# Gate and up as seven products per pair of chunks instead of eight, residual kept in DRAM

## What is computed

```
x = _layernorm(x + attn(x, Wq, Wk, Wv, Wo))
Wg = (gate_w - 128) * gate_scale[:, None]      # Wu and Wd in the same way
g = einsum('bsh,ih->bsi', x, Wg)
u = einsum('bsh,ih->bsi', x, Wu)
h = silu(g) * u
x = _layernorm(x + einsum('bsi,hi->bsh', h, Wd))
```

## Time and profile before

| | us |
|---|---|
| median of 3 runs (1772.68 to 1777.62) | 1775.47 |
| the profiled execution | 1769.1 |
| its span, slowest core | 1767.6 |
| TensorE busy in it | 1736.1 |
| VectorE, GpSimd, ScalarE busy | 545.4, 328.2, 263.8 |
| first gate/up half, with the wait at its start | 444.5 |
| second gate/up half | 441.9 |

### The profile page before, as it was taken

The page is one execution under the profiler, slowest core; times in us unless marked ns, Lnnn a source line. Parts: engine busy times, 40 slices in busy tenths (PEclk is TensorE's granted clock), DMA queues, the critical chain, the costliest instruction groups (busy, mean ns, idle before and its releaser), DMA issues.

```text
span 1767.6 us, 22037 instructions; the slowest of 8 cores (1762.0 to 1767.6 us)
## 1 busy us (share of the span) xinstructions
PE 1736.1 (98%) x8156; PEld 790.6 (45%) x8156; DVE 545.4 (31%) x950; ACT 263.8 (15%) x469; POOL 328.2 (19%) x459
## 2 busy tenths in 40 slices
PE   6999999999999999999999999999999999999997
...
PEclk9999999999999999999999999999999999999999
...
GB/s 145 179 95 143 143 144 161 171 178 118 85 83 78 78 72 73 83 76 106 25 90 122 81 74 36 73 82 77 79 72 72 83 78 106 23 138 155 51 72 119
DMA packets 146503, 173.27 MB, mean 98 GB/s; under 512 B 107872, under 2 KB 110048, under 8 KB 146272
## 3 DMA queue, kind: packets, MB, share of 16 engines
...
q10 hardware_dynamic: 144, 0.26, 0.0%
HBM read 266.21 MB, written 8.39 MB: 155 GB/s over the span
## 4 chain that ended last, share of the span: by engine, by line
PE 92%; DMA 3%; SPq 2%; POOL 1%; DVE 1%; issue 1%; ACT 0%; DVEq 0%; ACTq 0%; POOLq 0%
PE ps L324 25%; PE ps L336 25%; PE ps L354 20%; PE ps L379 5%; PE ps L303 4%; PE ps L267 4%; SPq L794 2%; DMA wk<-wk_os 2%; PE ps L255 2%; PE ps L192 2%; PE ps L284 2%; PE ps L237 1%; PE ps L239 1%; PE ps L200 1%; PE ps L214 1%; PE ps L206 1%
## 5 line engine op out<-in xcount | busy, mean ns | idle before, releaser
L324 PE MATMUL ps<-y1T,wgu 128*128 128x512 bf16 x2048 | 462.9, 379 | 2.2 <-DMA y1T<-y1b 2.2
L336 PE MATMUL ps<-y1T,wgu 128*128 128x512 bf16 x2048 | 462.9, 379 | 0.0
L324 PEld LDWEIGHTS ps<-y1T,wgu 128*128 128x128 bf16 x2048 | 200.3, 98 | 244.1 <-issue 2.6
L336 PEld LDWEIGHTS ps<-y1T,wgu 128*128 128x128 bf16 x2048 | 200.3, 98 | 241.8
L659 ACT ACTIVATE sil<-ps,gus 128x512 f32<-128x512 f32 x128 | 87.8, 687 | 1004.9 <-PE ps L324 775.9
L354 PE MATMUL ps<-wd,h_lo 128*128 128x512 bf16 x1024 | 222.4, 379 | 0.0
L506 DVE SCALAR_TENSOR_TENSOR h_hi<-ps,gus,sil 128x512 bf16<-128x512 f32 x64 | 48.0, 751 | 354.5 <-PE ps L336 354.5
L354 PEld LDWEIGHTS ps<-wd,h_lo 128*128 128x128 bf16 x1024 | 100.0, 98 | 121.1 <-issue 0.4
L506 DVE SCALAR_TENSOR_TENSOR h_lo<-ps,gus,sil 128x512 bf16<-128x512 f32 x64 | 48.1, 751 | 343.2 <-PE ps L336 342.4
L747 POOL DMA_DIRECT2D wgu<-wu_is x62 | 32.8, 528 | 641.7 <-PE ps L324 619.6
L354 PE MATMUL ps<-wd,h_hi 128*128 128x512 bf16 x640 | 139.4, 379 | 0.0
...
## 6 DMA issues: line engine op xcount, KB each, us to landing
wgu<-wg_is POOLq DMA_DIRECT2D x64, 512.0 KB, 6.1
wgu<-wu_is POOLq DMA_DIRECT2D x64, 512.0 KB, 5.1
wd<-wd_bs POOLq DMA_DIRECT2D x52, 512.0 KB, 5.4
wq<-wq_os POOLq DMA_DIRECT2D x16, 512.0 KB, 33.9
wo<-wo_bs POOLq DMA_DIRECT2D x16, 512.0 KB, 7.3
...
y<-Sx SPq DMA_DIRECT2D x14, 512.0 KB, 2.8
wdf<-wd_bs POOLq DMA_DIRECT2D x12, 512.0 KB, 9.1
```

Of the source, the lines that this page charges most:

```text
L324: mm = t.matmul(bank(2 * (u % 4)), wgu[(2 * i) % 5][:, 128 * k:128 * k + 128], y1T[:, T * k + 512 * tt:T * k + 512 * tt + 512], start=(k = ...
L336: mm = t.matmul(bank(2 * (u % 4) + 1), wgu[(2 * i + 1) % 5][:, 128 * k:128 * k + 128], y1T[:, T * k + 512 * tt:T * k + 512 * tt + 512], st ...
```

## The change

**Seven products.** Two chunks, 2p and 2p+1, are a pair; with the two token halves (tiles 0 to 3 and 4 to 7) and the two halves of the 2,048 input features (columns 0 to 1023 and 1024 to 2047) gate and up are each a product of 2x2 blocks. Eight block products are replaced by seven on sums and differences of blocks (Strassen's scheme in the form with shared sums). A block product has 8 matmuls instead of 16 for a full one. `pair(p)` has 14 products, x = 0 to 13, seven for gate and seven for up in turn (m = 0 and 1), each in bank (14p+x) mod 8.

**Token sums.** `y1T` is replaced by seven tensors: yB11 and yB22 (blocks), yD21 and yD12 (differences), ySc, ySb and ySa (sums of tiles j and j+4). The normed tiles are written as 128x1024 pieces: ScalarE writes a block (`stg`) and norms one half of `Sx` in place, VectorE norms the other half, GpSimd subtracts (L996), and VectorE and GpSimd then make twelve sums `sts`. SyncE transposes 28 pieces of 1,024 columns instead of 8 of 2,048.

**Weight sums.** Slabs stay in bf16 with 128 subtracted, so their sums are whole numbers that bf16 holds exactly. For each pair VectorE centers four slabs `raw` and makes six sums of 128x1024 (`sum_q`, `sum_r`, `sum_p`) for the next pair, GpSimd four differences (`dif_v`, `dif_u`); they go round in twelve buffers `cmb`.

**Result sums.** ScalarE copies products 0, 1, 4 and 5 into SBUF (`x4`, `x3`), VectorE adds the others to them from PSUM (`c21`, `c12`, `e4`, `c11`, `c22`, two each), GpSimd makes the sums between (`s34`, `f11_f22`, six of 128x512 f32), ScalarE the four `sil`, and VectorE the four `h` blocks (`hprod`), now with both inputs in SBUF.

**Buffers.** Since the sums need space, the normed residual is written to a DRAM scratch `y1s` by ScalarE's queue after the norm, is read and rewritten in 128x512 pieces (`ybk`) during the first down part by SyncE's queue, and is read back into SBUF (`Sy`) after the second gate/up half. The down slabs have four buffers, which are the four `raw` of the odd pairs. In `down` TensorE waits for h step by step.

```diff
+    y1s = nc.dram_tensor("y1s", [NQT, 128, D], F32)
...
+    wd = [at(f"wd{i}", 2048, BF16, raw_off[4 + i] * KB) for i in range(4)]
...
+            def product(p, x, w, y):
+                for k in range(8):
+                    mm = t.matmul(bank((14 * p + x) % 8), w[:, 128 * k:128 * k + 128],
+                                  y[:, 512 * k:512 * k + 512], start=(k == 0), stop=(k == 7))
+                mm.then_inc(pe_m, 1)
+
+            def pair(p):
+                for m in range(2):
+                    t.wait_ge(ve_cw, 4 * p + m + 1)
+                    empty(p, m)
...
+                    product(p, m, raw[rslot(p, m, 1)][:, 1024:2048], yD21)
...
+                for m in range(2):
+                    t.wait_ge(po_cb, 4 * p + 2 + m + 1)
+                    empty(p, 12 + m)
...
+                    product(p, 12 + m, cmb[cslot(p, QU, m)], ySa)
...
+            def sum_q(p, m):
+                v.wait_ge(ve_cw, 4 * p + m + 1)
+                cfree(v, p, QQ + m)
+                v.tensor_tensor(cmb[cslot(p, QQ, m)][:, :], quarter(p, m, 2, 1), quarter(p, m, 2, 2),
+                                ALU.add).then_inc(ve_cb, 1)
...
+            def e4(p, m):
+                v.wait_ge(pe_m, 14 * p + 8 + m + 1)
+                v.wait_ge(po_s34, 2 * p + m + 1)
+                v.tensor_tensor(x4[m][:, :], x4[m][:, :], bank((14 * p + 8 + m) % 8), ALU.add).then_inc(ve_e, 1)
...
+            def hpair(p, slab):
+
+                more = p + 1 < NP
+                if more:
+                    cen(p + 1, 0)
+                    cen(p + 1, 1)
+                    sum_q(p + 1, 0)
+                    sum_q(p + 1, 1)
+                c21(p, 0)
+                c21(p, 1)
+                hprod(p, 0)
...
+                hprod(p, 2)
+                if slab is not None:
+                    cen_wd(slab)
+                c22(p, 0)
...
+            def s34(p, m):
+                g.wait_ge(ac_s3, 2 * p + m + 1)
+                g.wait_ge(ve_c21, 2 * p + m + 1)
+                g.tensor_tensor(x4[m][:, :], x4[m][:, :], x3[m][:, :], ALU.add).then_inc(po_s34, 1)
+
+            def f11_f22(p, m):
+                g.wait_ge(ve_e, 2 * p + m + 1)
+                g.wait_ge(ve_c12, 2 * p + m + 1)
+                g.wait_ge(po_s34, 2 * p + m + 1)
+                g.tensor_tensor(x3[m][:, :], x4[m][:, :], y12[m][:, :], ALU.subtract).then_inc(po_f11, 1)
+                g.wait_ge(po_f11, 2 * p + m + 1)
+                g.tensor_tensor(x4[m][:, :], x4[m][:, :], y21[m][:, :], ALU.subtract).then_inc(po_f22, 1)
+
+            def sums(p):
+                dif_v(p, 0)
+                dif_v(p, 1)
+                dif_u(p, 0)
+                s34(p, 0)
+                s34(p, 1)
+                dif_u(p, 1)
+                f11_f22(p, 0)
+                f11_f22(p, 1)
+
+            def slabs_free(p):
+
+                g.wait_ge(pe_m, 14 * p + 6)
+                g.wait_ge(ve_cb, 6 * p + 6)
+                g.wait_ge(po_cb, 4 * p + 4)
...
+            for p in range(HP):
+                sums(p)
+                slabs_free(p)
+                if p < HP - 1:
+                    for x in range(4):
+                        gu(p + 2, x)
+            for w in range(WA):
+                wds(w)
...
+            for d in range(4):
+                for j in range(NQT):
+                    if d > 0:
+                        sy.wait_ge(st_yb[j // 4], 64 * d)
+                    sy.dma_start(ybk[j][:, :], y1s[j, :, 512 * d:512 * d + 512]).then_inc(ld_yb, 16)
+                for j in range(NQT):
+                    sy.wait_ge(ve_da, 8 * d + j + 1)
+                    sy.dma_start(y1s[j, :, 512 * d:512 * d + 512], ybk[j][:, :]).then_inc(st_yb[j // 4], 16)
```

More of the change, by code:

```diff
@@ L342, in down @@
+            def down(lo, hi, q):
                 for d in range(lo, hi):
```

554 lines of the change are left out of this document (385 added, 169 removed).

## The result

The changed kernel takes 1850.3 us (median of 4 runs, 1849.0 to 1851.2), the kernel before 1775.1 beside it: ratio 1.0423, 95% interval 1.0405 to 1.0441. It is slower by 75 us. In some executions the cores of one die show a lower granted clock and take longer; the ratios leave these out, and so do the times given for e2_memset and e5_slab_early, two each.

A forecast was written before the change was run, and what follows sets the result against it. The kernel before was taken as bound by TensorE, the changed one by VectorE and GpSimd excluding each other. 1769.1 + 59.9 + 31.1 = 1860.1, with 5 added 1865 us; range 1728 to 1925, the forecast's own 1812 to 1925.

The forecast's parts named there:

- case (e): The forecast itself: a gate/up pair takes 28 to 31 us, slower, 1812 to 1907 us, likeliest 1865; chance 0.60.
- A pair of 29.6 us: Gate/up: VectorE and GpSimd exclude each other and bind a pair in turn at 29.6 us; TensorE idles a fifth.
- rival (b): Gate/up: GpSimd's bf16 difference takes 1.27 us, not 2.4; pair 25.2 us, time 1728 to 1733; chance 0.10.
- (d): Gate/up: VectorE's bf16 sum takes 1.2 us, not 0.61; pair 33 us, time 1960; chance 0.08.
- each one that waits going next: Pair layout: VectorE and GpSimd alternate, giving 29.6 us; 26.1 if VectorE's consecutive instructions keep their turn, 30.8 if GpSimd's do.
- (c): Gate/up: VectorE keeps its turn in runs; pair 26.1 us, time 1755 to 1760; chance 0.10.
- Second half, +31.1: Second gate/up half: 5 us down tail, 15 pairs (444), last pair 24; 473 against 441.9 us.
- First half, +59.9: First gate/up half: pair 0 ends at +57, 14 pairs of 29.6, last pair 33; 504.4 against 444.5 us.
- The waits for the first down slab: Last pair of each gate/up half: down slabs come late; first down matmul at 33 us, in the second half 24.
- (a): Gate/up: no exclusion that matters, TensorE stays the bound at 24.2 us a pair; time 1688 to 1693; chance 0.12.
- The idle costs nothing more: Gate/up: despite TensorE's idle time the granted clock stays at nine tenths or more of 2.4 GHz; no added time.
- The residual's trips: Start and down stages: the residual's DRAM traffic costs nothing; if cover goes, one wait of some 5 us in second down.

The follow-up runs named there:

- e2_memset: Changed kernel with GpSimd's four weight differences per pair replaced by memsets of the same tiles, differences left out of the result: 1820.5 and 1814.9 us, ratio 1.0245.
- e5_slab_early: Changed kernel with the next pair's or first down slabs issued by GpSimd before `f11_f22` instead of behind it: 1800.4 and 1801.0 us.
- e10: e5_slab_early with each GpSimd weight difference replaced by two memsets in a row, differences left out of the result: 1730.5 us, ratio 0.9739.
- e4: Changed kernel with the norm's one-element product `nm` rewritten to have one SBUF tensor input: 1852.3 us, ratio 1.0438.
- e7: e6_all with VectorE's order in the first pair rewritten, pair 0's combinations and h products ahead of centering pair 1's slabs: 1732.7 us, ratio 0.9750.
- e11: e7 with two of pair 1's four slabs held back behind the ySa transposes: 1727.3 us, ratio 0.9711.
- e3_dif_dve: Changed kernel with the four weight differences of a pair made by VectorE instead of GpSimd: 1797.1 us, ratio 1.0125.
- e9: Changed kernel with the residual's loads for the second down stage issued block by block, not all at once: 1854.4 us, ratio 1.0441.
- e6_all: Changed kernel with weight differences on VectorE, slabs issued before f11/f22, the norm's product with one tensor input, and residual loads block by block: 1725.0 us, ratio 0.9708.

## Why the prediction was right, and which of its steps were not

The time (1850.3 against 1865), the sign and the case (e) came out. The parts came out less well. In the spans, 80.8 us more where the sum had 91.0, the forecast has the start of the first half 28 us too short and the down stretches 14, the pairs of the first half 17 us too long and the second half 33. That this comes to 10 us in all is luck; that VectorE and GpSimd, held by each other, would bind the pair above 26.6 us is not. TensorE is busy for 80% of the first gate/up half, as forecast, and for 90% of the second.

**A pair of 29.6 us: mechanism right, size 2 us too high.** e10 beside e5_slab_early shows the exclusion to be the cause and not the load. GpSimd's bf16 difference is 2.12 to 2.17 us free (I took 2.4, rival (b) had 1.27), VectorE's bf16 sum 0.64 a piece (0.61; (d) is gone), an instruction with a PSUM input is never held (L638: 1.27 for two beside L1018; all 320 result sums of the kernel take 0.67 to 0.69). What failed is the rule of turns in my layout, "each one that waits going next". The three differences run through in 6.4 us where I had them alternate with two centerings and a sum for 8.8. The fourth difference stands beside c12, which isn't held, where I had charged 2.9 us for it. In other places turns do alternate: in e5_slab_early the centering gets in between differences, and so does an h product that comes 0.3 us before the end of one. What decides who goes next the runs don't show. So 27.5 to 28.4 us, between (c) and (e). The same layout with such runs would have been 26.1 or 30.8 by my own words, and neither is it.

**Second half, +31.1: wrong, -2.2.** In steps from the issue of the slabs behind one f22 to the next: to the first of them 30.1 us (I had 32), 13 pairs of 27.5 instead of 29.6 (-27 us), the tail 52.2 instead of 56.2. Nearly all of it is the pair's size: at 27.5 us the pair of seven products costs what the 128 matmuls cost before, 27.6.

**First half, +59.9: +70.6.** Same steps: to the first issue behind f22 82.7 us (510.64, from 427.9), where I had 54 (2.6 before the end of pair 0 at +57): **+28**. Then 14 periods of 28.4 instead of 29.6, -17, and the tail 35.2 against 35.6. The start is the step that failed, in three terms that the clock shows:

```profile
446.97 12.19 POOL L1002 TENSOR_TENSOR sts<-Sx,Sx 128x1024 bf16<-128x1024 f32 x4
...
470.99 0.56 POOL L973 DMA_DIRECT2D raw<-wg_is  x1 [11.82 <-DMA ySb<-sts]
...
490.14 3.21 DVE L500 TENSOR_TENSOR cmb<-raw 128x1024 bf16<-128x1024 bf16 x2 [6.78 <-DMA ySa<-sts]
```

The norm ended at +19 and not +5, since nm of six of the eight tiles is held by a GpSimd difference (5.3 us a tile at the end). The slabs of pair 1 were issued at +43 and not +25: the sums of the two engines hold each other (3.05 us one on GpSimd, I had 2.4), and the transposes run one by one behind them. And `sum_q` of pair 1 waits for the ySa transposes (+62), because its buffers are theirs; this wait wasn't in my list at all. What the first term is worth stays open, since e4 hardly shortened the norm; e7 and e11 show the last one, the ySa landing, on TensorE's path once the order within pair 0 isn't, though it came 5 to 10 us later there.

**The waits for the first down slab**, 33 and 24 us into the last pair, came out (13.3 us of wait at 943.0). e5 shows what a wrong place of four issues costs: its early issue takes 31 us from the first half and 22 from the second, because I had looked at the slab's landing only at the ends. In the sum it is the second loop, 25.9 us, hidden under 27.5: costed at nothing rightly, but it is the reason why the rivals (a) and (b) could not have come true as priced. e2_memset and e3_dif_dve, which take away the differences' holds (not those of the f32 sums), end at 1797 to 1820 us; by these (a) would have been nearer to 1800 than to 1693.

**"The idle costs nothing more": wrong.** The granted clock is 0.93 over the first half, and TensorE is busy 412.1 us in it against 395.0 in the second, for the same 1,792 matmuls. Behind the waits of 8.7 and 22.0 us, 16 matmuls take 5.5 and 5.7 us instead of 3.62, which is on the way to the lower of the two levels (1.2 GHz of 2.4); behind two shorter waits in pairs 1 and 2 it is the same:

```profile
453.67 5.48 PE L361 MATMUL ps<-yD,raw 128*128 128x512 bf16 x16 [8.71 <-DMA yD<-stg]
...
494.20 5.70 PE L361 MATMUL ps<-ySb,cmb 128*128 128x512 bf16 x16 [22.02 <-DVE y L625]
526.06 5.13 PE L361 MATMUL ps<-ySb,cmb 128*128 128x512 bf16 x16 [3.69 <-DVE y L625]
555.25 5.30 PE L361 MATMUL ps<-ySb,cmb 128*128 128x512 bf16 x16 [2.28 <-DVE y L625]
```

That is 1.5 to 2.1 us for each of them. Among the pairs of the first half the clock falls six times in this way, among those of the second once; behind most of their waits, such as the 1.4 us at 1382.21, the matmuls go on at 3.62 us for 16. How much of the 17 us the time pays isn't shown, since TensorE isn't the bound within the pairs.

**The residual's trips and the down stretches, at nothing: wrong for the second, +11.4.** 4.7 us are waits for tmp, where VectorE's evacuation is behind; 6.4 are matmuls of 389 ns instead of 379 (640 of them, clock 0.96) behind the stretch's late start. Of the burst of loads e9 shows a part of some 2 us. e6_all, without the burst and with a clean start of the stretch, still takes 146.3 against 138.2, with 4.5 us waits for tmp and a DMA share of 0.84; what delays VectorE there is open. In the first down stretch the +2.8 us are the clock's: behind the wait of 13.3 us its first 66 matmuls take 17.35 us instead of 14.4.
